# Laying k over its rows with 0/1 matmuls on four row tiles, in the projection of a fused attention and feed-forward layer

## The chip, the cores and the metric

The kernel runs on one core of a Trainium2 chip. The metric is the device time of one execution in microseconds (us); lower is better. Engine names are those of the profile: PE is TensorE (its weight loads are PEld), DVE is VectorE, ACT is ScalarE, POOL is GpSimd, and SP is SyncE, which here only issues DMAs (SPq is its queue).

## What is computed

The reference, cut to what matters here; the feed-forward half is only named.

```python
# x: (1, 4096, 256), 16 heads of 16
q = rope(x @ Wq.T + bq)         # per head; rope turns neighbouring features by a position's angle
k = rope(x @ Wk.T + bk)
v = x @ Wv.T + bv
p = softmax(q @ k.T / 16)       # per head, 4096 x 4096
x = layernorm(x + (p @ v) @ Wo.T)
x = layernorm(x + ffn(x))       # three gated and plain layers of width 1024
```

All of it is float32. Where a matmul is to be fast, an operand is split into a high part, rounded to the fp32r type, and a low part, the rest, and the products high by high, high by low and low by high are summed, as rows of one contraction.

## The kernel before

It has three stages that follow each other: `project`, `attend` and `feed_forward`. The change is in `project` and in the first waits of `attend`.

`project` goes over the sequence in NCH = 8 chunks of CH = 512 columns. A chunk has four items: q and k of feature half 0, then q and k of half 1 (item n, with t = n % 2 for q or k). For an item PE makes a 128x512 product into a PSUM bank `ps`, ACT adds the bias and writes `item[b]`, DVE swaps neighbouring rows into `pair` (a stream shuffle), multiplies `item` by the cosine table, POOL multiplies `pair` by the sine table, DVE adds the two (`rotated`), casts the sum to the high part (`high`) and subtracts to get the low part (`low`). After its four items a chunk's v is made: four token tiles, each two 128x256 float32 matmuls and a third with one row of ones that adds the bias of v.

What `attend` needs of k is `k_all`: for each pair of heads, 64 rows per head, in which rows 0 to 15 hold the high part, 16 to 31 the low part, 32 to 47 the high part again, and three rows of ones stand at 48 to 50 (`K_PART`, `SHIFT_ROW`). In the kernel before, SP stores both parts of q and of k into a DRAM tensor (`store`), and reads k's back into the three places per head (`place_k`: 6 DMAs for each chunk and half). The rows of ones are written by two DMAs at the start of `attend`. q is read back from DRAM later, in `attend`, by `place_q`.

The engines are separate programs, written as in-order lists with semaphores; nothing but these waits sets the order. DVE's `high` waits until the store that last used its `parts` buffer has landed (`parts_free`, line 288), SP's `place` waits for the landing of k's store, and SP's load of the next x and tables waits for `v_ready` and stands behind the chunk's stores and places on SP's list. PE's chunk waits for its x (`x_in`). `project` ends with SP's wait for all stores and for the places of k but the last, which `attend` issues.

`attend` begins with the `wide` matmuls (line 521) and DVE's maxima over them (line 710): these need the first q tile (`q_in`) and k.

Of the kernel before, what the change touches and what calls it, by code (L numbers as in the profile page):

```python
# [58 lines left out]
PLACES = PAIR * len(K_PART)  # L59


def place_k(sp, k_parts, k_all, c, ft, done):
    cols = bass.ds(c * CH, CH)
    pairs = slice(ft * PAIRS // FT, (ft + 1) * PAIRS // FT)
    for e in range(PAIR):
        for r, part in enumerate(K_PART):
            src = k_parts[part].rearrange("(j e d) s -> e d j s", e=PAIR, d=HD)[e]
            at = e * HALF + r * HD
            sp.dma_start(k_all[at:at + HD, pairs, cols].bitcast(F32), src[:, pairs, cols]).then_inc(done, 16)
# [10 lines left out]
def project(nc, io, parts_dram, v_all, k_all):  # L80

# [6 lines left out]
    with ExitStack() as ctx:  # L88
# [9 lines left out]
        RING = 4  # L98
# [3 lines left out]
        bv_sb = sb("b_v", [1, D])  # L102
        one_row = sb("one_row", [1, P])
        xt = [sb(f"xt{p}", [P, FT, CH]) for p in range(2)]
        table = [sb(f"table{p}", [P, 2, CH]) for p in range(2)]
        item = [sb(f"item{b}", [P, CH]) for b in range(RING)]
        pair = [sb(f"pair{b}", [P, CH]) for b in range(2)]
        parts = [sb(f"parts{b}", [P, 2, CH], F32R) for b in range(2)]
        ps = [psum(f"ps_qk{b}", [P, CH]) for b in range(RING)]
        psv = [psum(f"ps_v{a}", [P, 2, D]) for a in range(2)]  # L110

        w_in = sem("w_qk_in")
# [11 lines left out]
        low_done = sem("low_done")  # L124
        parts_free = [sem(f"parts_free{b}") for b in range(2)]
        k_in = sem("k_in")
        v_ready = sem("v_ready")
        v_free = sem("v_free")
        waited = sem("project_waited")
        sp_waited = sem("sp_waited")  # L130
        ones_set = sem("ones_set")

        ITEMS = 2 * FT
        TOTAL = NCH * ITEMS

        def started(n):

            return not isinstance(n, int) or 0 <= n < TOTAL

        block = ctx.enter_context(nc.Block())  # L140

        @block.sync
        def _(sp):
            def load(p, c):
                cols = bass.ds(c * CH, CH)
# [17 lines left out]
            def chunk(c, first=False):  # L163
                store(c, 0)
                if not first:
                    place(c - 1, 1)
                store(c, 1)
                store(c, 2)
                place(c, 0)
                store(c, 3)  # L170

            sp.dma_start(w_sb[:, 0], io["wqT"].rearrange("(t p) o -> p t o", p=P)).then_inc(w_in, 16)
            load(0, 0)
# [3 lines left out]
            sp.wait_ge(w_in, 16)  # L177
            sp.dma_start(w_sb[:, 1], io["wkT"].rearrange("(t p) o -> p t o", p=P)).then_inc(w_in, 16)
            sp.dma_start(wv_sb[:], io["wvT"].rearrange("(t p) o -> p t o", p=P)).then_inc(v_weights_in, 16)
            sp.dma_start(bv_sb[:], io["bv"].rearrange("(o d) -> o d", o=1)).then_inc(v_weights_in, 16)  # L180
            load(1, 1)
            chunk(0, first=True)
            sp.wait_ge(v_ready, 2)
            load(0, 2)
            chunk(1)
            sp.wait_ge(v_ready, 4)
            load(1, 3)
            with sp.Fori(1, NCH // 2 - 1) as cc:
                for p in range(2):
                    chunk(cc * 2 + p)  # L190


                    sp.wait_ge(v_ready, (cc * 2 + p + 1) * 2)
                    load(p, cc * 2 + p + 2)
            chunk(NCH - 2)
            chunk(NCH - 1)
            for b in range(2):
                sp.wait_ge(parts_free[b], 16 + 16 * TOTAL // 2)
            sp.wait_ge(k_in, 16 * PLACES * (NCH * FT - 1))

        @block.gpsimd
        def _(pool):
            pool.memset(v_all[:, :, :, :, HD:HD + 1], 1.0).then_inc(ones_set, 1)
            pool.wait_ge(ones_set, 1)
            pool.memset(one_row[:], 1.0).then_inc(ones_set, 1)
            pool.wait_ge(ones_set, 2)
            with pool.Fori(0, NCH // 2) as cc:
                for p in range(2):
                    pool.wait_ge(table_in[p], cc * 32 + 32)
                    for m in range(ITEMS):  # L210
                        n = (cc * 2 + p) * ITEMS + m

                        pool.wait_ge(swapped, n + 1)
                        pool.tensor_tensor(pair[m % 2][:], pair[m % 2][:], table[p][:, 1], ALU.mult).then_inc(sine_done, 1)

        @block.tensor
        def _(pe):
            def chunk(c, p):
                for m in range(ITEMS):
                    ft, t = m // 2, m % 2  # L220
                    n = c * ITEMS + m
                    if isinstance(c, int) and c == 0 and m < 2:

                        pe.wait_ge(w_in, 16 * (t + 1))
                    if started(n - RING):

                        pe.wait_ge(biased, n - RING + 1)
                    for i in range(FT):
                        last = pe.matmul(ps[m][:], w_sb[:, t, i, ft * P:(ft + 1) * P], xt[p][:, i],  # L229
                                         start=(i == 0), stop=(i == FT - 1))  # L230
                    last.then_inc(projected, 1)
                if isinstance(c, int) and c == 0:
                    pe.wait_ge(v_weights_in, 32)
                    pe.wait_ge(ones_set, 2)
                for a in range(2):

                    pe.wait_ge(v_free, c * 2 + a + 1)
                    for b in range(2):
                        tt = 2 * a + b
                        for i in range(FT):  # L240
                            pe.matmul(psv[a][:, b], xt[p][:, i, tt * P:(tt + 1) * P], wv_sb[:, i],
                                      start=(i == 0), stop=False)
# [4 lines left out]
            for p in range(2):  # L247
                pe.wait_ge(x_in[p], 16)
                chunk(p, p)
            with pe.Fori(1, NCH // 2) as cc:  # L250
                for p in range(2):
                    pe.wait_ge(x_in[p], cc * 16 + 16)
                    chunk(cc * 2 + p, p)

        @block.scalar
        def _(act):
            def chunk(c):
                for m in range(ITEMS):
                    ft, t = m // 2, m % 2
                    n = c * ITEMS + m  # L260
                    act.wait_ge(projected, n + 1)

                    act.wait_ge(low_done, n + 1)
                    act.activation(item[m][:], ps[m][:], ACT.Identity, bias=b_sb[:, t, ft:ft + 1]).then_inc(biased, 1)
                    if m >= ITEMS - 2:

                        a = m - (ITEMS - 2)
                        act.wait_ge(v_ready, c * 2 + a + 1)
                        for b in range(2):
                            dst = v_all[:, :, bass.ds(c * TT + 2 * a + b, 1), :, 0:HD]  # L270
                            last = act.activation(dst.rearrange("p g a j d -> p (g a) j d"),
                                                  psv[a][:, b].rearrange("p (g j d) -> p g j d", g=NG, j=HG), ACT.Copy)
                        last.then_inc(v_free, 1)

            act.wait_ge(b_in, 32)
            chunk(0)
            chunk(1)
            with act.Fori(2, NCH) as c:
# [1022 lines left out]
```

## Time and profile before

| what | value |
|---|---|
| median of 3 runs | 3553.01 us (3552.21 to 3554.25) |
| the profiled execution's own time | 3551.05 us |
| its span in the trace | 3549.4 us |
| mean granted clock of PE | 0.971 |
| busy: PE, DVE, ACT, POOL | 3414.3, 2997.2, 2451.1, 242.7 us |
| first matmul of `attend` | at 178.32 us |

The span is what the trace covers; the time is measured around it and is 1.65 us more. Every moment below is counted from the start of the span. The projection is the first twentieth of the span, and is the only stretch in which the DMA engines are nearly full; the page's forty slices of some 89 us each show that as the first two.

### The profile page before, as it was taken

To read this page: it belongs to the slowest core of one execution; us is meant where nothing else is said; L and a number is where in the kernel's file an instruction comes from. 1 tells how busy PE (TensorE), PEld (TensorE's weight loads), DVE (VectorE), ACT (ScalarE), POOL (GpSimd) and SP (SyncE) were. 2 spreads that over 40 slices of the span, in tenths; PEclk is the share of its full clock that TensorE was granted. 3 is DMA by queue.
4 is the path that set the end of the run, shared out by engine and by line. 5 is a ranking of instruction groups with operands and counts; after the bars stand their busy time and mean duration, and the time that the engine had idled before them with its cause. 6 is when DMAs were issued, how large, how long until landed. Compare 5 with 4: busy or idle time off the path is not lost. (4 is left out here: it accounts for less than half of the span.)

```text
span 3549.4 us, 67886 instructions
## 1 busy us (share of the span) xinstructions
PE 3414.3 (96%) x28122; PEld 1560.8 (44%) x28122; DVE 2997.2 (84%) x3204; ACT 2451.1 (69%) x4472; POOL 242.7 (7%) x440
## 2 busy tenths in 40 slices
PE   8569999999999999999999999999999699999998
PEld 3223333333333333333333333333333388888887
DVE  6599999999999999999999999999994245555554
ACT  2108888888888888888888888888889422222222
POOL 3300000000000000000000000000000011111100
PEclk8759999999999999999999999999999799999999
DMA  8920000000000010001000000000000501111100
GB/s 211 222 36 12 16 14 14 25 13 13 14 30 18 12 62 13 14 13 61 18 17 25 15 14 14 14 14 13 17 8 5 187 31 37 37 37 37 37 19 13
DMA packets 64150, 126.12 MB, mean 36 GB/s; under 512 B 13447, under 2 KB 25800, under 8 KB 62648
## 3 DMA queue, kind: packets, MB, share of 16 engines
q1 hardware_dynamic: 54920, 102.49, 10.3%
q0 software_dynamic: 8928, 19.35, 1.9%
q8 instruction: 221, 3.62, 0.4%
q14 instruction: 81, 0.66, 0.1%
HBM read 90.59 MB, written 41.16 MB: 37 GB/s over the span
## 5 line engine op out<-in xcount | busy, mean ns | idle before, releaser
L710 DVE TENSOR_REDUCE group_max<-wide 128x2 f32<-128x1024 f32 x2048 | 2473.0, 1222 | 23.9 <-PE wide L521 17.2
L681 ACT ACTIVATE probs<-scores 128x512 f32<-128x512 f32 x4046 | 2202.9, 600 | 291.8 <-PE scores L606 43.9
L547 PE MATMUL sums<-probs,v_all 128*17 128x256 f32 (+1 forms) x16120 | 1277.9, 389 | 7.7 <-ACT mixed L664 6.8
L606 PE MATMUL scores<-q_sb,k_all 51*128 51x512 f32 x3968 | 989.0, 495 | 6.7 <-ACT probs L681 5.7
L521 PE MATMUL wide<-k_all,q_sb 48*128 48x512 f32 x4096 | 850.6, 411 | 52.4 <-DVE group_max L710 26.7
L606 PEld LDWEIGHTS scores<-q_sb,k_all 51*128 51x128 f32 x3968 | 370.9, 183 | 843.5 <-ACT probs L681 830.0
L547 PEld LDWEIGHTS sums<-probs,v_all 128*17 128x17 f32 x16120 | 267.1, 95 | 748.1 <-issue 365.8
L521 PEld LDWEIGHTS wide<-k_all,q_sb 48*128 48x128 f32 x4096 | 397.8, 191 | 91.0 <-DVE group_max L710 63.9
L1083 ACT ACTIVATE whole_hid<-acc,scale 128x512 f32<-128x512 f32 x128 | 84.7, 689 | 321.7 <-PE acc L964 316.9
L964 PE MATMUL acc<-hid_b,h2T 128*128 128x512 f32 x1024 | 241.6, 396 | 0.0
L964 PE MATMUL acc<-hid_a,h1T 128*128 128x512 f32 x1024 | 240.2, 394 | 0.0
L964 PEld LDWEIGHTS acc<-hid_b,h2T 128*128 128x128 f32 x1024 | 192.3, 188 | 46.4
L964 PEld LDWEIGHTS acc<-hid_a,h1T 128*128 128x128 f32 x1024 | 191.6, 187 | 47.3
L1173 DVE CAST hid_a<-whole_hid 128x512 fp32r<-128x512 f32 x128 | 54.4, 425 | 185.7 <-ACT whole_hid L1083 183.5
L1074 ACT ACTIVATE gate<-acc,scale 128x512 f32<-128x512 f32 x64 | 44.1, 690 | 125.9 <-PE acc L964 125.9
L229 PE MATMUL ps_qk<-xt,w_qk 128*128 128x512 f32 x128 | 72.6, 729 | 27.7 <-DMA xt<-in_xT 27.6
L1175 DVE TENSOR_TENSOR hid_a<-whole_hid,hid_a 128x512 fp32r<-128x512 f32 x128 | 88.6, 692 | 4.4
L1182 DVE SCALAR_TENSOR_TENSOR whole_hid<-acc,scale,gate 128x512 f32<-128x512 f32 x64 | 48.1, 751 | 44.9 <-PE acc L964 44.9
L937 PE MATMUL tok<-wo,heads_sb 128*128 128x256 f32 x256 | 59.3, 392 | 17.8 <-DVE heads_sb L1148 17.8
L964 PE MATMUL acc<-x1t,w1T 128*128 128x512 f32 x256 | 71.8, 402 | 2.1 <-DVE x1t L1167 2.1
L1173 DVE CAST hid_b<-whole_hid 128x512 fp32r<-128x512 f32 x64 | 27.1, 424 | 55.1 <-ACT whole_hid L1083 55.0
L483 POOL CAST shift_parts<-shift 16x128 bf16<-16x128 f32 x32 | 8.9, 279 | 932.7 <-ACT shift L673 896.7
(89 smaller groups left out, 1295.0 us busy)
## 6 DMA issues: line engine op xcount, KB each, us to landing
k_all<-k_parts SPq DMA_DIRECT2D x96, 128.0 KB, 5.1
q_sb<-q_parts SPq DMA_DIRECT2D x192, 64.0 KB, 2.8
q_parts<-parts SPq DMA_DIRECT2D x16, 512.0 KB, 5.9
k_parts<-parts SPq DMA_DIRECT2D x16, 512.0 KB, 6.3
heads<-mixed SPq DMA_DIRECT2D x32, 256.0 KB, 2.6
heads_sb<-heads SPq DMA_DIRECT2D x8, 1024.0 KB, 4.9
shares<-shares_dram POOLq DMA_DIRECT2D x112, 64.0 KB, 2.3
xt<-in_xT SPq DMA_DIRECT2D x8, 512.0 KB, 6.3
```

The source lines that it names most:

```text
L229: last = pe.matmul(ps[m][:], w_sb[:, t, i, ft * P:(ft + 1) * P], xt[p][:, i], start=(i == 0), stop=(i == FT - 1))
L521: last = pe.matmul(wide[n % 2][:, e], q_sb[g][rows, j, t * P:(t + 1) * P], k_all[rows, g * GP + j, b * CH:(b + 1) * CH], start=True, stop= ...
L547: last = pe.matmul(sums[32 * j:32 * j + HD + 1, cols], v_all[:, g, kt, j], probs[(kt * HG + j) % RING][:, cols], start=(kt == 0 and cols.s ...
L606: pe.matmul(scores[(s + e) % BANKS][:], k_all[rows, g * GP + j, n // HG * P:(n // HG + 1) * P], q_sb[g][rows, j], start=True, stop=True).t ...
L681: act.activation(probs[n % RING][:], bank, ACT.Exp, scale=INV_SCALE)\
L710: dve.reduce_max(group_max[:, n], wide[n % 2][:], AX_X).then_inc(wide_free, 1)
L937: last = pe.matmul(tok[t // 2][:, t % 2], heads[:, g, t * P:(t + 1) * P], wo[:, g], start=(g == 0), stop=(g == NG - 1))
L964: mm = pe.matmul(dst, w.bitcast(view), src[h].bitcast(view), start=(first and h == 0), stop=(last and h == 1))
L1083: act.activation(whole[o % 4][:], acc[n % 4][:], ACT.Gelu, scale=scale[:, 2 + layer, o:o + 1])\
L1173: dve.tensor_copy(dst[0][:, k % HT], whole[k % 4][:]).then_inc(rounded, 1)
L1175: dve.tensor_tensor(dst[1][:, k % HT], whole[k % 4][:], dst[0][:, k % HT].bitcast(F32), ALU.subtract)\
L1182: dve.scalar_tensor_tensor(out=whole[o % 4][:], in0=acc[(2 * o + 1) % 4][:], scalar=scale[:, 1, o:o + 1], in1=gate[o % 2][:], op0=ALU.mult ...
```

## The change

`store` and `place_k` for k are gone, with k's DRAM tensor and the DMAs that wrote rows of ones. Instead PE lays k over its rows. A 0/1 matrix `choose` (32 rows by 128 columns for each of four pairs, for each of the two parts) says which row goes where; for each chunk and half (`spread_k`) PE runs eight fp32r matmuls of 128x512, two (high and low part) for each of four pairs, each with 32 rows, on the four row tiles of the array, into four PSUM banks. ACT copies each bank into `k_all`, adding a column `ones_rows` that is 1 in the three rows of ones. The k parts that the matmuls read lie in a stretch of `k_all` that is written last (`lent`).

Further: `ps` has two banks and not four; v's matmuls stand in the middle of a chunk, after items 0 and 1, and v's bias is one fp32r matmul with 128 rows (`two_rows`, `bv_parts`: high and low part of the bias) where a float32 matmul with one row stood; ACT copies v by one instruction for two token tiles; the high part is a tensor_tensor maximum of the item with itself and not a cast; the addition and the high part of item n come one item later on DVE, after the shuffle and cosine of item n + 1; the low part of q goes to POOL; all loops of `project` are written out; `v_all` has its axes in another order.

```diff
-            def store(c, m):
-
-                ft, t = m // 2, m % 2
-                sp.wait_ge(low_done, RING + c * ITEMS + m + 1)
-                dst = parts_dram[t].rearrange("a f s -> f a s")[ft * P:(ft + 1) * P]
-                sp.dma_start(dst[:, :, bass.ds(c * CH, CH)], parts[t][:].bitcast(F32)).then_inc(parts_free[t], 16)
-
-            def place(c, ft):
-
-                sp.wait_ge(parts_free[1], 16 + (c * FT + ft + 1) * 16)
-                sp.sem_inc(sp_waited, 1)
-                place_k(sp, parts_dram[1], k_all, c, ft, k_in)
...
+            for c in range(NCH):
+                for ft in range(FT):
+
+                    i = c * FT + ft
+                    sp.wait_ge(low_q, i + 1)
+                    dst = q_dram.rearrange("a f s -> f a s")[ft * P:(ft + 1) * P]
+                    sp.dma_start(dst[:, :, c * CH:(c + 1) * CH], parts[0][i % 2].bitcast(F32)).then_inc(q_stored[i % 2], 16)
+                if c + 2 < NCH:
+
+                    sp.wait_ge(v_ready, 2 * c + 2)
+                    sp.wait_ge(projected, (c + 1) * ITEMS)
+                    sp.wait_ge(rotated, (c + 1) * ITEMS)
+                    load(c + 2)
...
+            def spread_k(c, ft):
+                i = c * FT + ft
+                if i == 0:
+                    pe.wait_ge(choose_set, 5)
+
+                pe.wait_ge(low_k, i + 1)
+                if i > 0:
+
+                    pe.wait_ge(spread_free, JP * i)
+                for a in range(2):
+                    for j in range(JP):
+                        rows = slice(j * ROWS, (j + 1) * ROWS)
+                        last = pe.matmul(spread[j][:], choose[rows, a], parts[1][i % 2][rows, a],
+                                         start=(a == 0), stop=(a == 1))
+                        if a == 1:
+                            last.then_inc(spread_ready, 1)
+
+            for c in range(NCH):
+
+                pe.wait_ge(x_in[c % 2], (c // 2 + 1) * 16)
+                item_of(c, 0)
+                item_of(c, 1)
+                values(c)
+                if c > 0:
+                    spread_k(c - 1, 1)
+                item_of(c, 2)
+                item_of(c, 3)
+                spread_k(c, 0)
+            spread_k(NCH - 1, 1)
...
-                        last = pe.matmul(psv[a][:, b], one_row[:], bv_sb[:], start=False, stop=True)
+                        last = pe.matmul(psv[a][:, b], two_rows[:], bv_parts[:], start=False, stop=True)
...
+                for j in range(JP):
+
+                    act.wait_ge(spread_ready, i * JP + j + 1)
+                    act.activation(k_all[:, ft * JP + j, c * CH:(c + 1) * CH], spread[j][:], ACT.Identity,
+                                   bias=ones_rows[:]).then_inc(spread_free, 1)
...
+                dve.tensor_tensor(parts[t][i % 2][:, 0], item[n % RING], item[n % RING], ALU.max).then_inc(high_done, 1)
...
+                if n % 2 == 1:
+                    low(n - 1)
...
-            place_k(sp, k_parts, k_all, NCH - 1, FT - 1, k_in)
...
-            pe.wait_ge(k_ones, 16 * PAIR)
```

How the engines' lists look, at three places. PE in the kernel before, at the start of its first chunk (`ps_qk` are the items, `ps_v` is v):

```order
L229 MATMUL ps_qk<-xt,w_qk 128x512 x8
L241 MATMUL ps_v<-w_v,xt 128x256 x2
L244 MATMUL ps_v<-b_v,one_row 128x256
L241 MATMUL ps_v<-w_v,xt 128x256 x2
L244 MATMUL ps_v<-b_v,one_row 128x256
```

PE in the changed kernel, from the end of v in its second chunk on (`ps_spread` is k laid over its rows):

```order
L226 MATMUL ps_v<-b_v_parts,two_rows 128x256
L241 MATMUL ps_spread<-k_all,choose 128x512 x8
L208 MATMUL ps_qk<-xt,w_qk 128x512 x4
L241 MATMUL ps_spread<-k_all,choose 128x512 x8
L208 MATMUL ps_qk<-xt,w_qk 128x512 x4
L223 MATMUL ps_v<-w_v,xt 128x256 x2
```

The eight item matmuls of a chunk are now four and four, and behind each four and behind v stands work that needs what DVE has made of an earlier item.

ACT before, its first instructions after the table load:

```order
L264 ACTIVATE item<-ps_qk,b_qk 128x512 x3
L271 ACTIVATE v_all<-ps_v 128x4x4x16 x2
L264 ACTIVATE item<-ps_qk,b_qk 128x512
L271 ACTIVATE v_all<-ps_v 128x4x4x16 x2
L264 ACTIVATE item<-ps_qk,b_qk 128x512 x3
```

ACT in the changed kernel, its second chunk:

```order
L270 ACTIVATE item<-ps_qk,b_qk 128x512 x2
L277 ACTIVATE v_all<-ps_v 128x32x16 x2
L287 ACTIVATE k_all<-ps_spread,ones_rows 128x512 x4
L270 ACTIVATE item<-ps_qk,b_qk 128x512 x2
L287 ACTIVATE k_all<-ps_spread,ones_rows 128x512 x4
```

Four copies of k now stand on ACT ahead of the biases of items 2 and 3, and four more ahead of the next chunk's.

DVE before, for two items (item, cosine, high part of the item before, addition, low part of the item before):

```order
L305 STREAM_SHUFFLE pair<-item 128x512
L307 TENSOR_TENSOR item<-item,table 128x512
L289 CAST parts<-item 128x512
L311 TENSOR_TENSOR item<-item,pair 128x512
L294 TENSOR_TENSOR parts<-item,parts 128x512
```

DVE in the changed kernel, for an even item and the odd one after it:

```order
L354 STREAM_SHUFFLE pair<-item 128x512
L356 TENSOR_TENSOR item<-item,table 128x512
L310 TENSOR_TENSOR item<-item,pair 128x512
L321 TENSOR_TENSOR k_all<-item 128x512
L326 TENSOR_TENSOR k_all<-item,k_all 128x512
L354 STREAM_SHUFFLE pair<-item 128x512
L356 TENSOR_TENSOR item<-item,table 128x512
L310 TENSOR_TENSOR item<-item,pair 128x512
L321 TENSOR_TENSOR q_parts<-item 128x512
```

The low part of k (L326) is the fifth instruction of the iteration of the item after it, so that what PE lays out for a half of k waits for the bias of the next item.

## Rows read from the trace of the kernel before

In a row of stretches stand: from and to in us from the start of the span, its length, the busy us of PE, PEld, DVE, ACT and POOL (with the number of instructions), PE's granted clock as a share of full speed, the mean busy share of the 16 DMA engines, and GB/s.

**Rows 1.** Stretches of the span: two chunks of the projection, then the first maxima.

```profile
20.90:38.13 17.23, 13.68 (x41) 6.92 (x40) 15.64 (x26) 4.62 (x10) 7.19 (x5) 0.93 0.74 188
38.13:57.81 19.68, 15.83 (x40) 7.71 (x41) 13.31 (x26) 3.96 (x8) 7.08 (x4) 0.85 0.99 242
...
178.30:264.00 85.70, 59.34 (x151) 21.62 (x151) 84.71 (x78) 0.27 (x1) 2.95 (x7) 0.50 0.20 35
```

**Rows 2.** Waits from 0 to 180 us: total, times, longest.

```profile
DVE parts L289 <- DMA k_parts<-parts: 34.9, 14, 3.6
PE ps_qk L229 <- DMA xt<-in_xT: 27.6, 7, 5.5
```

**Rows 3.** PE's timeline in the projection: start us, us, engine, line, operation, count.

```profile
5.53 8.90 PE L229 MATMUL ps_qk<-xt,w_qk 128*128 128x512 f32 x16 [5.53 <-DMA xt<-in_xT]
...
20.90 7.13 PE L229 MATMUL ps_qk<-xt,w_qk 128*128 128x512 f32 x16
...
29.45 1.13 PE L241 MATMUL ps_v<-w_v,xt 128*128 128x256 f32 x4
30.51 0.69 PE L244 MATMUL ps_v<-b_v,one_row 1*128 1x256 f32 x2
31.14 1.13 PE L241 MATMUL ps_v<-w_v,xt 128*128 128x256 f32 x4
...
38.14 9.29 PE L229 MATMUL ps_qk<-xt,w_qk 128*128 128x512 f32 x16 [3.56 <-DMA xt<-in_xT]
...
77.45 10.10 PE L229 MATMUL ps_qk<-xt,w_qk 128*128 128x512 f32 x16 [3.42 <-DMA xt<-in_xT]
...
97.53 8.61 PE L229 MATMUL ps_qk<-xt,w_qk 128*128 128x512 f32 x16 [3.43 <-DMA xt<-in_xT]
```

**Rows 4.** DVE's timeline of one item.

```profile
22.42 0.71 DVE L305 STREAM_SHUFFLE pair<-item 128x512 f32<-128x512 f32 x1
23.17 0.69 DVE L307 TENSOR_TENSOR item<-item,table 128x512 f32<-128x512 f32 x1
23.78 1.49 DVE L289 CAST parts<-item 128x512 fp32r<-128x512 f32 x1
25.19 0.68 DVE L311 TENSOR_TENSOR item<-item,pair 128x512 f32<-128x512 f32 x1
25.79 0.68 DVE L294 TENSOR_TENSOR parts<-item,parts 128x512 fp32r<-128x512 f32 x1
```

**Rows 5.** DVE's timeline of the last item, the second waiting for the first.

```profile
163.56 0.43 DVE L289 CAST parts<-item 128x512 fp32r<-128x512 f32 x1 [3.56 <-DMA k_parts<-parts]
164.02 0.69 DVE L294 TENSOR_TENSOR parts<-item,parts 128x512 fp32r<-128x512 f32 x1
```

**Rows 6.** Groups by line and form, 0 to 260 us: busy us, mean ns of one, idle before.

```profile
L214 POOL TENSOR_TENSOR pair<-pair,table 128x512 f32<-128x512 f32 x32 | 56.6, 1769 | 99.7 <-DVE pair L305 99.7
L264 ACT ACTIVATE item<-ps_qk,b_qk 128x512 f32<-128x512 f32 x32 | 22.0, 689 | 60.4 <-PE ps_qk L229 59.1 <-DVE parts L294 1.2
```

**Rows 7.** Timeline of the feed-forward stage: three ACT instructions back to back.

```profile
2890.15 1.85 ACT L1083 ACTIVATE whole_hid<-acc,scale 128x512 f32<-128x512 f32 x3 [16.49 <-PE acc L964]
```

**Rows 8.** PE's timeline in attention: two pairs of fp32r matmuls, each pair on two row tiles.

```profile
600.28 0.50 PE L606 MATMUL scores<-q_sb,k_all 51*128 51x512 f32 x2
600.61 0.40 PE L521 MATMUL wide<-k_all,q_sb 48*128 48x512 f32 x2
600.94 0.63 PE L547 MATMUL sums<-probs,v_all 128*17 128x256 f32 x8
```

**Rows 9.** Timeline of the hand-over: the last store, the first q loads, the first matmul of attention.

```profile
166.28 0.43 SPq L155 DMA_DIRECT2D k_parts<-parts  x1
...
172.87 2.66 SPq L77 DMA_DIRECT2D q_sb<-q_parts  x6
...
178.32 1.22 PE L521 MATMUL wide<-k_all,q_sb 48*128 48x512 f32 x4 [25.76 <-DMA q_sb<-q_parts]
```

**Rows 10.** The page's DMA issues: size of one, median us from issue to landing.

```profile
k_parts<-parts SPq DMA_DIRECT2D x16, 512.0 KB, 6.3
```

More of the change, by code:

```diff
@@ L58 @@
 SLOT = SHIFT_ROW + 3
[L59 to L69, printed above, removed]
+PLACES = PAIR * len(Q_PART)
 def place_q(sp, q_parts, q_sb, c, g, done):
@@ L163, in chunk @@
[L163 to L173, printed above, removed]
+            sp.dma_start(w_sb[:, 0], io["wqT"].rearrange("(t p) o -> p t o", p=P)).then_inc(w_in[0], 16)
+            load(0)
@@ L181, in _ @@
[L181 to L196, printed above, removed]
+            for at in (0, ROWS):
+                sp.dma_start(bv_sb[at:at + 1], io["bv"].rearrange("(o d) -> o d", o=1)).then_inc(v_weights_in, 16)
@@ L216, in _ @@
+            for n in range(TOTAL):
+                c = n // ITEMS
+                if n % ITEMS == 0:
+                    pool.wait_ge(table_in[c % 2], (c // 2 + 1) * 32)
+                pool.wait_ge(swapped, n + 1)
+                pool.tensor_tensor(pair[n % 2], pair[n % 2], table[c % 2][:, 1], ALU.mult).then_inc(sine_done, 1)
+                if n % 2 == 1:
+                    low(n - 1)
         @block.tensor
         def _(pe):
[L218 to L234, printed above, removed]
@@ new lines, in item_of @@
+            def item_of(c, m):
+                ft, t, n = m // 2, m % 2, c * ITEMS + m
+                if c == 0 and m < 2:
+                    pe.wait_ge(w_in[t], 16)
+                if n >= BANKS:
+                    pe.wait_ge(biased, n - BANKS + 1)
+                for i in range(FT):
+                    last = pe.matmul(ps[n % BANKS][:], w_sb[:, t, i, ft * P:(ft + 1) * P], xt[c % 2][:, i],
+                                     start=(i == 0), stop=(i == FT - 1))
+                last.then_inc(projected, 1)
@@ L255, in _ @@
+            for c in range(NCH):
[3 more added lines that the diff above has]
+                values(c)
+                if c > 0:
+                    spread_k(c - 1, 1)
[3 more added lines that the diff above has]
+            spread_k(NCH - 1, 1)
         @block.scalar
         def _(act):
[L257 to L273, printed above, removed]
@@ L275, in _, with bias @@
-            act.wait_ge(b_in, 32)
-            chunk(0)
-            chunk(1)
-            with act.Fori(2, NCH) as c:
-                chunk(c)
-            act.wait_ge(v_free, 2 + 2 * NCH)
+            def bias(c, m):
+                ft, t, n = m // 2, m % 2, c * ITEMS + m
+                if n == RING - 2:
+                    act.wait_ge(bv_set, 3)
+                if n >= RING:
+                    act.wait_ge((low_q, low_k)[t], (n - RING) // 2 + 1)
+                act.wait_ge(projected, n + 1)
+                act.activation(item[n % RING], ps[n % BANKS][:], ACT.Identity, bias=b_sb[:, t, ft:ft + 1]).then_inc(biased, 1)
@@ L282, in _ @@
+            act.wait_ge(b_in, 32)
+            for c in range(NCH):
+                bias(c, 0)
+                bias(c, 1)
+                values(c)
+                if c > 0:
+                    spread_k(c - 1, 1)
+                bias(c, 2)
+                bias(c, 3)
+                spread_k(c, 0)
+            spread_k(NCH - 1, 1)
+            act.wait_ge(v_free, 2 * NCH)
+            act.wait_ge(spread_free, NCH * FT * JP)
         @block.vector
         def _(dve):
-            def high(n, b):
-                if started(n):
-                    dve.wait_ge(rotated, n + 1)
-                    dve.wait_ge(parts_free[b % 2], (n - b % 2) * 8 + 16)
-                    dve.tensor_copy(parts[b % 2][:, 0], item[b][:]).then_inc(high_done, 1)
@@ L291, in low, with rotate @@
-            def low(n, b):
-                if started(n):
-                    dve.wait_ge(high_done, n + 1)
-                    dve.tensor_tensor(parts[b % 2][:, 1], item[b][:], parts[b % 2][:, 0].bitcast(F32), ALU.subtract)\
-                        .then_inc(low_done, 1)
-            def chunk(c, p):
+            def rotate(n):
+                dve.wait_ge(cosine_done, n + 1)
+                dve.wait_ge(sine_done, n + 1)
+                dve.tensor_tensor(item[n % RING], item[n % RING], pair[n % 2], ALU.add).then_inc(rotated, 1)
@@ new lines, in high, with low @@
+            def high(n):
+                t, i = n % 2, n // 2
+                dve.wait_ge(rotated, n + 1)
+                if i >= 2 and t == 0:
+                    dve.wait_ge(q_stored[i % 2], 16 * (i // 2))
+                if i >= 2 and t == 1:
+                    dve.wait_ge(spread_ready, JP * (i - 1))
+                dve.tensor_tensor(parts[t][i % 2][:, 0], item[n % RING], item[n % RING], ALU.max).then_inc(high_done, 1)
+            def low(n):
+                k = parts[1][n // 2 % 2]
+                dve.wait_ge(high_done, n + 1)
+                dve.tensor_tensor(k[:, 1], item[n % RING], k[:, 0].bitcast(F32), ALU.subtract).then_inc(low_k, 1)
@@ L315, in _ @@
-            dve.sem_inc(v_free, 2)
-            for b in range(2):
-                dve.sem_inc(parts_free[b], 16)
-            for p in range(2):
-                dve.wait_ge(table_in[p], 32)
-                chunk(p, p)
-            with dve.Fori(1, NCH // 2) as cc:
-                for p in range(2):
-                    dve.wait_ge(table_in[p], cc * 32 + 32)
-                    chunk(cc * 2 + p, p)
-            high(TOTAL - 1, (TOTAL - 1) % RING)
-            low(TOTAL - 1, (TOTAL - 1) % RING)
```

169 lines of the change are left out of this document (97 added, 72 removed).

## The prediction

> **What bounds the kernel now.** The execution read here took 3551.05 us, 1.65 us more than its span, and lies 1.96 us under the median of the runs (3553.01). A measurement of this kernel can tell about 0.2%, some 7 us, from no change. The first question is which part of the span the change can reach. The stretches answer it: up to 152 us PE makes the projection, at 178.32 comes the first matmul of attention [rows 9], and from there on DVE is busy 84.71 of 85.70 us with its maxima [rows 1], an operation that the diff leaves alone. So I look for one number, the moment of that first matmul; all behind it moves by as much.
>
> Next, what a chunk of the projection lasts and why. The stretch from one chunk's first matmul to the next's is 19.68 us for the third chunk, with the DMA engines busy 0.99, PE 15.8, DVE 13.3 and ACT 4 us [rows 1]; three chunks in a row, from 38.14 to 97.53, take 19.8 us each [rows 3]. The waits name the same cause: DVE waits 34.9 us for the landing of k's stores, PE 27.6 us for x [rows 2]. One chunk shows the kernel before transfers crowd it: from 20.90 to 38.13, DMA share 0.74, 17.23 us, and 3.56 of these are PE's wait for x [rows 1, 3]. The projection is bound by its transfers, and a chunk without that bound needs 13.7 us of PE at full clock.
>
> Then the clock. It is 0.85 in such a stretch: after each wait of 3.4 to 3.9 us PE is at the lower of its two levels (1.2 GHz) for a while. A chunk's items take 7.13 us at 2.4 GHz (from 20.90) and 9.29, 10.10 and 8.61 after a wait [rows 3]; over the six chunks that begin after a wait the mean is 9.45. So a wait costs its own length and 2.3 us more.
>
> **What the change takes away.** Per chunk k's store is 1 MB (two of 512 KB [rows 10]) and its places are 1.5 MB, beside 1 MB of q's store and 1 MB of x and tables: 4.5 MB become 2. At the 240 GB/s of a full stretch that is 19 us before and 8.5 after. Transfers stop being the bound. Against that no term of the old chunk is left standing, so I build the new one from PE's list.
>
> **PE's work per chunk, at full clock.** Four items: one is a quarter of 7.13, that is 1.72 from start to start, 3.44 for two. v: per token tile the two matmuls take 1.06 (29.45 to 30.51) and the bias 0.63 (30.51 to 31.14) [rows 3]. The new bias matmul is fp32r with 128 rows; no such form is in the trace. It costs more than nothing and less than 0.63; the nearest row is one of the four records of 1.06, 0.265, and I take 0.25. v is then 4 x 1.31 = 5.24. Laying k out: eight matmuls on four row tiles. The nearest rows are pairs on two row tiles in attention: scores to wide and wide to sums are 0.33 us each for two matmuls of 512 columns [rows 8]. If four tiles run together, the eight cost 2 x 0.33 = 0.66; if only two do, 4 x 0.33 = 1.32; below 0.5 I see no reason, and I take 0.75, with something for changing the array's layout. Twice per chunk. Sum: 3.44 + 5.24 + 0.75 + 3.44 + 0.75 = 13.62 us, nearly what it was (13.7).
>
> Here a rule stands against the change. The rows with a one-row matmul among full ones already show such a price: 0.63 where the same columns with 128 rows take 0.53 [rows 3], so 0.1 us per change of layout, and my 0.75 holds that once. The Trainium skill, "TensorEngine Tiling (Array Packing)", section Key Properties, says that changing the tiling mode drains TensorE; by that the price would be paid going in and coming out, and the sum would be about 1.6 us longer over sixteen lays.
>
> **PE's new wait.** The order list puts the lay-out of a half right behind items 2 and 3, and it needs `low_k` of item 1. That is made on DVE in the iteration of item 2, which needs item 2's bias, and this stands on ACT behind four copies of k. From the end of the lay-out before items 2 and 3: 0.3 us until the first copy starts; four copies, one each 0.58 us (three in 1.85 us: (1.85 - 0.69) / 2 [rows 7]), 2.32; the bias 0.69 [rows 6] and 0.1 for its signal; then DVE: shuffle 0.75 and cosine 0.61 from start to start [rows 4], addition and high part 0.72 each, since each now waits for the one before (0.69 and a step of 0.03, as in [rows 5]), low part 0.69, with its signal 0.8. That is 0.3 + 2.32 + 0.79 + 3.6 = 7.0 us, under which PE has 3.44 us of items. PE waits about 3.6 us per chunk, and behind it in its list stands everything, the next chunk's items first. The wait for x is gone, but one of the same length takes its place. After a wait of 3.4 us the clock fell in each case seen, so I add the same 2.3 us. Period: 13.62 + 3.63 + 2.3 = 19.55 us, against 19.7 before.
>
> What else is on the lists hides under that. DVE per two items: two shuffles and cosines 2.72, two additions and high parts 2.9, one low part 0.7: 6.3, per chunk 12.6 of 19.6 us. The cast's 1.49 us [rows 4] goes, without gain, as DVE waits anyway; if the new form takes 1.49 too, the critical one before `low_k` does, and PE waits 0.8 us longer, 6 us in all. POOL does three instructions of 1769 ns [rows 6] per two items, 10.6 us per chunk; it would need 3.2 us each to matter. ACT: fourteen instructions of at most 0.69, 9.7 us. The loads of x are issued a chunk ahead and land in some 6 us; q's stores have their own buffers. The memsets and small DVE instructions of the start lie under the landing of the weights: I take v's first matmul at 11 us.
>
> **The sum.** First matmul at 5.53 as now. First chunk: items until 10.4, v until 16.2, items until 19.7, wait 3.2, lay-out: 18.5 us, so 24.0. Six chunks of 19.6: 141.6. Last chunk: 12.8 of PE, 2.3 for the clock, wait 3.7, a lay-out at the low clock 1.5, again a wait of 3.7 for the last low part, a lay-out 1.5, four copies 2.5: 28.0, so 169.6. Hand-over: before, the last store was issued at 166.28, with 6.3 us to landing [rows 10] that is 172.6 to 173.0, and the first q load was issued at 172.87 [rows 9]; I take 0.5. Then 5.45 us from the first q load to the first matmul (172.87 to 178.32), as before. That gives 175.6, where it was 178.32: 2.7 us earlier. 3551.05 - 2.7 = 3548.3, and with 1.96 for the median 3550.3 us. The change gives its own gain back through the new wait; what is left is the hand-over, in which k's last store no longer lands.
>
> **Rivals.**
> *A, likeliest: same within 0.2%.* The sum with the bounds of its small terms. The clock rises at moments that have to do with when the wait ends, and a chunk's loss was 1.5 us (8.61) to 3.0 us (10.10 [rows 3]); over eight chunks that is 6 us down or up. Chance 0.46, own range 3546 to 3560.
> *B, faster: the clock holds.* Items, v and lay-outs are denser than before, since no one-row matmul is among them. Then 2.3 us x 8 = 18 less: 3532. Against it: all seven waits of 3.4 us and more in the trace were followed by 1.2 GHz. Chance 0.12.
> *C, faster: small terms at their low ends.* Bias 0.15 and lay-out 0.6: 0.4 + 0.3 us per chunk, 5.6 us; with a wait of 3.3, 2.4 more: 3542. Chance 0.21. The Trainium skill's "TensorE: Matmul & The Clock Gate", Part 3, gives a speedup of 3.07 for four row tiles with 512 columns, which would favour this over two tiles at a time; no row of the trace has four tiles, so it changes no number here.
> *D, slower: row tiles do not run together.* At two at a time a lay-out costs 1.32, 0.57 more, and twice that at 1.2 GHz, where the one after the wait lies: 8 x (0.57 + 1.14) = 14 us: 3564. It decides from 1.0 us per lay-out on. Fully one after another (2.6) would be 3590. Chance 0.12.
> *E, slower: the wait is longer.* The new form of high part takes 1.49, or ACT's copies 0.69 each in a row: 0.4 to 0.8 us per chunk, up to 6 more, and a clock that rises later in every chunk: 3561. Chance 0.09.
> That the change does nothing since k's transfers were hidden is excluded for its first half by [rows 2]; what remains of it is A, in which their place is taken.
>
> **The numbers.** Faster (B, C) 0.33, same 0.46, slower (D, E) 0.21. The range takes A with C and most of D and E: 3538 to 3563.
>
> **What would show it.** In the changed kernel's stretches the DMA share of the projection falls to about 0.4. PE's waits name `low_k` (DVE's low part) once a chunk, 3 to 4 us, not x; its clock is again near 0.85. The period between two chunks' first matmuls is 19 to 20.5 us; a lay-out of eight takes 0.6 to 0.8 at 2.4 GHz; the fp32r bias 0.2 to 0.3; the high part 0.69. The first matmul of attention stands near 175.6. The prediction is wrong if PE's wait is under 2 us, if the clock stays up through it, or if the eight lay-out matmuls take more than 1 us.

## The result and the profile after

The changed kernel takes 3545.53 us (median of 20 runs, 3542.66 to 3549.1), the kernel before 3550.44 us in its 20 runs. The ratio is 0.9984, with a 95% interval of 0.9977 to 0.9991: some 5 us faster, within 0.2%, and clear of zero. The prediction was 3550 us (3538 to 3563) with "same" as the likeliest case. One execution of the kernel fill below took 5752.86 us and is left out of its median.

The profiled execution has a span of 3544.4 us where the kernel before had 3549.4. Its first matmul of attention is at 173.89 us where it was at 178.32 [rows 9]; behind it DVE is busy 84.73 of 85.70 us, as before [rows 1].

The timeline of PE in the changed kernel shows a chunk as a whole (start us, us, engine, line, operation, count, and the wait before it):

```profile
62.10 5.01 PE L208 MATMUL ps_qk<-xt,w_qk 128*128 128x512 f32 x8
...
67.92 1.03 PE L223 MATMUL ps_v<-w_v,xt 128*128 128x256 f32 x4
68.60 0.47 PE L226 MATMUL ps_v<-b_v_parts,two_rows 128*128 128x256 f32 x1
68.91 1.03 PE L223 MATMUL ps_v<-w_v,xt 128*128 128x256 f32 x4
...
70.97 0.74 PE L241 MATMUL ps_spread<-k_all,choose 32*128 32x512 f32 x8
71.64 3.70 PE L208 MATMUL ps_qk<-xt,w_qk 128*128 128x512 f32 x8
79.77 1.23 PE L241 MATMUL ps_spread<-k_all,choose 32*128 32x512 f32 x8 [4.43 <-DVE k_all L326]
80.92 5.83 PE L208 MATMUL ps_qk<-xt,w_qk 128*128 128x512 f32 x8
```

Read from item to item: the eight matmuls of items 0 and 1 take 5.0 to 5.8 us, v 0.98 us per token tile (67.92 to 68.91; 1.08 for the last one, which the lay-out follows), the lay-out behind it 0.67 (70.97 to 71.64), items 2 and 3 3.70; then PE waits 4.43 us for the low part of k, and the lay-out after the wait takes 1.15 (79.77 to 80.92). From 62.10 to 80.92 is 18.8 us. The six periods from 23.44 to 138.12 have a mean of 19.1 us. In the kernel before PE waited for x at this point [rows 2, 3].

Two of the waits from 0 to 176 us, as in [rows 2]:

```profile
PE ps_spread L241 <- DVE k_all L326: 39.4, 9, 5.7
...
PE ps_qk L208 <- DMA xt<-in_xT: 5.5, 1, 5.5
```

All of PE's waits for x but the very first are gone, 39.4 us for DVE's low part have come. The stretch of that chunk (columns as in [rows 1]):

```profile
62.10:80.92 18.82, 14.39 (x56) 7.76 (x52) 16.82 (x23) 8.68 (x14) 9.61 (x7) 0.86 0.33 112
```

The DMA engines are busy 0.33 where they were at 0.99, the clock is where it was (0.86, before 0.85), and DVE is busy 16.8 of 18.8 us. That last figure I had not expected: my sum had 12.6. DVE's and POOL's timelines at one place, where DVE ends one item and makes the next up to its low part:

```profile
90.92 0.69 DVE L356 TENSOR_TENSOR item<-item,table 128x512 f32<-128x512 f32 x1
91.53 1.76 DVE L310 TENSOR_TENSOR item<-item,pair 128x512 f32<-128x512 f32 x1
93.32 0.69 DVE L321 TENSOR_TENSOR q_parts<-item 128x512 fp32r<-128x512 f32 x1
94.48 0.01 DVE L354 LOAD_MASK_SELECT pair<-item  x1 [0.47 <-ACT item L270]
94.50 0.73 DVE L354 STREAM_SHUFFLE pair<-item 128x512 f32<-128x512 f32 x1
95.27 0.69 DVE L356 TENSOR_TENSOR item<-item,table 128x512 f32<-128x512 f32 x1
95.88 1.75 DVE L310 TENSOR_TENSOR item<-item,pair 128x512 f32<-128x512 f32 x1
97.66 0.69 DVE L321 TENSOR_TENSOR k_all<-item 128x512 fp32r<-128x512 f32 x1
98.39 0.69 DVE L326 TENSOR_TENSOR k_all<-item,k_all 128x512 fp32r<-128x512 f32 x1
```

```profile
90.97 1.77 POOL L193 TENSOR_TENSOR pair<-pair,table 128x512 f32<-128x512 f32 x1 [2.73 <-DVE pair L354]
94.10 1.27 POOL L186 TENSOR_TENSOR q_parts<-item,q_parts 128x512 fp32r<-128x512 f32 x1 [1.36 <-DVE q_parts L321]
95.33 1.75 POOL L193 TENSOR_TENSOR pair<-pair,table 128x512 f32<-128x512 f32 x1
```

The addition (L310), 0.68 us before [rows 4], takes 1.76: it begins while POOL multiplies by the sine table (90.97 to 92.74) and ends 0.55 us after POOL does. The shuffle beside POOL's low part (94.50) keeps its 0.73. PE and ACT at the same place, up to the lay-out that needs this low part:

```profile
91.27 3.70 PE L208 MATMUL ps_qk<-xt,w_qk 128*128 128x512 f32 x8
99.13 1.23 PE L241 MATMUL ps_spread<-k_all,choose 32*128 32x512 f32 x8 [4.16 <-DVE k_all L326]
...
91.38 2.42 ACT L287 ACTIVATE k_all<-ps_spread,ones_rows 128x512 fp32r<-128x512 f32 x4
93.67 0.70 ACT L270 ACTIVATE item<-ps_qk,b_qk 128x512 f32<-128x512 f32 x1
```

ACT's four copies do stand ahead of the bias of item 2 (93.67), but DVE has no time for that item before 94.01, when it ends the item before: it waits only 0.47 us for the bias.

The hand-over, in the timelines of ACT, SP and PE:

```profile
164.86 2.42 ACT L287 ACTIVATE k_all<-ps_spread,ones_rows 128x512 fp32r<-128x512 f32 x4 [4.58 <-PE ps_spread L241]
...
167.77 7.33 SPq L67 DMA_DIRECT2D q_sb<-q_parts  x16
...
173.89 1.22 PE L547 MATMUL wide<-k_all,q_sb 48*128 48x512 f32 x4 [9.16 <-DMA q_sb<-q_parts]
```

### The profile page after: what moved, and what is told of

It reads as the page before. It is cut to its first block and busy times, and to the rows that moved or that the text cites. A ratio compares the mean times of both kernels' runs of the same rounds, so it can differ in the third digit from the quotient of the medians.

```text
span 3544.4 us, 67661 instructions
## 1 busy us (share of the span) xinstructions
PE 3408.5 (96%) x28218; PEld 1563.6 (44%) x28218; DVE 3024.8 (85%) x3196; ACT 2488.0 (70%) x4520; POOL 263.8 (7%) x458
```

## The experiments

Ten kernels, each timed beside the kernel before on the same chip (its medians there 3550.3 to 3550.8 us); ratios are to those. Behind them stands a table with the first matmul of attention of each. Savings in us are against the changed kernel's 3545.53 unless the text says otherwise.

**1. Idle matmuls in PE's wait (fill).** The wait stays, but PE is busy in it.

```diff
+                if ft == 0:
+                    pe.wait_ge(v_free, c * 2 + 1)
+                    for _ in range(4):
+                        pe.matmul(psv[0][:].rearrange("p a d -> p (a d)"), w_sb[:, 0, 0, 0:P],
+                                  wv_sb[:].rearrange("p a d -> p (a d)"), start=True, stop=True)
                 pe.wait_ge(low_k, i + 1)
```

> The changed kernel with four float32 matmuls of 512 columns (0.86 us each at 2.4 GHz, 3.4 us) put on PE ahead of each lay-out of a chunk's first half, where PE waits 4.2 us; they write a bank that nobody reads. Theory: the wait costs its length and, through the clock, some 2 us for the items and 0.5 for the lay-out after it. With the wait filled the clock stays at 2.4 GHz, the wait itself stays (DVE's chain sets it): the period from chunk to chunk falls from 19.2 to about 16.8 us, the first matmul of attention comes 17 us sooner (near 157), the time is near 3528 where the changed kernel has 3545.5. Rival: the period is set by DVE or the copies and PE's clock is only a companion: no change, 3545.

Measured: 3534.92 us (median of five), ratio to before 0.9956 (0.9943 to 0.9969): 10.6 us less, where the theory had 17. In its trace of PE:

```profile
70.27 3.60 PE L237 MATMUL ps_v<-w_v,w_qk 128*128 128x512 f32 x8
74.87 0.74 PE L246 MATMUL ps_spread<-k_all,choose 32*128 32x512 f32 x8 [1.00 <-DVE k_all L331]
75.54 3.70 PE L208 MATMUL ps_qk<-xt,w_qk 128*128 128x512 f32 x8
```

After the filled wait the lay-out takes 0.67 and the items 3.70 us, in every chunk, where they took 1.1 and 5.6; the clock is 1.00 from 60 to 120 us. So the clock's part is shown: work that computes nothing saves 10.6 us. The period is 17.6 and not 16.8 us, though. From 22.67 to 128.41 DVE is busy 101.65 of 105.74 us, and it waits once a chunk, for 0.17 us:

```profile
83.56 0.72 DVE L359 STREAM_SHUFFLE pair<-item 128x512 f32<-128x512 f32 x1
84.31 0.69 DVE L361 TENSOR_TENSOR item<-item,table 128x512 f32<-128x512 f32 x1
84.92 1.76 DVE L315 TENSOR_TENSOR item<-item,pair 128x512 f32<-128x512 f32 x1
...
92.36 0.72 DVE L359 STREAM_SHUFFLE pair<-item 128x512 f32<-128x512 f32 x1
```

Two items in 8.8 us (83.56 to 92.36), 17.6 per chunk: with PE's clock up, DVE with its slow additions is the bound. The rival is half right.

**2. Lay-outs one chunk later (later).** On PE, and alike on ACT:

```diff
                 item_of(c, 1)
+                if c > 0:
+                    spread_k(c - 1, 0)
                 values(c)
                 if c > 0:
                     spread_k(c - 1, 1)
                 item_of(c, 2)
                 item_of(c, 3)
-                spread_k(c, 0)
```

> The changed kernel with both lay-outs of a chunk one chunk later, the first behind items 0 and 1 and the second behind v of the next chunk, on PE and on ACT alike. Theory: PE's wait for the low part of k is gone; DVE becomes the bound, with 8.3 us per two items (its addition takes 1.76 us while POOL works), 16.6 us per chunk; PE is busy 13.3. The first matmul of attention comes 12 to 17 us sooner, 3530. Rival: what bounds a chunk is DVE plus the transfer between engines in any order, then under 4 us: 3543.

Measured: 3543.67 us, 0.9982 (0.9973 to 0.9991), 1.9 us under the changed kernel, whose own runs lie apart by more. My theory fell. PE's wait did not go but moved behind v:

```profile
86.56 0.69 DVE L325 TENSOR_TENSOR k_all<-item 128x512 fp32r<-128x512 f32 x1
87.29 0.69 DVE L330 TENSOR_TENSOR k_all<-item,k_all 128x512 fp32r<-128x512 f32 x1
...
88.03 1.22 PE L241 MATMUL ps_spread<-k_all,choose 32*128 32x512 f32 x8 [3.95 <-DVE k_all L330]
89.19 9.52 PE L208 MATMUL ps_qk<-xt,w_qk 128*128 128x512 f32 x16
```

With its slow additions DVE needs some 17.6 us per chunk (fill), PE 12.2 at full clock. So PE waits in this order too, again in one piece, of 3.6 to 4.0 us, and the clock falls behind it (items 9.52 for 7.13); the period stays at 19.1 us. With more than one wait per chunk it can be otherwise (later_act, below).

**3. The bias of item 2 ahead of ACT's copies (bias2).**

```diff
                 values(c)
+                bias(c, 2)
                 if c > 0:
                     spread_k(c - 1, 1)
-                bias(c, 2)
                 bias(c, 3)
```

> The changed kernel with the bias of item 2 ahead of ACT's four copies of k's second half. My sum had 2.3 us of copies in PE's wait; if that holds the wait falls from 4.2 to under 2.5 us and the time by 13 us or more, since the clock gains too. Rival, from the trace after: DVE is busy until 0.3 us before that bias arrives, because its additions take 1.76 us, so the copies cost only 0.3 us per chunk: 3543, no change that can be told.

Measured: 3543.14 us, 0.9978 (0.9969 to 0.9987); PE's waits are 3.8 to 4.4 us, as they were. The 2.3 us of copies that my sum had in the wait cost next to nothing, as the rival had it: in the changed kernel DVE waits 0 to 0.94 us per chunk for the bias behind them, and it is not free earlier. That the median is 2.4 us lower is within what its runs lie apart. (Its profiled execution, with a span of 3549.4 us, lies above its median, so it is read here for the waits alone.)

**4. The kernel before without k's transfers (no_k).** What the removed transfers were worth by themselves. In their place `k_all` is filled by ACT with copies of a weight tile, and the waits for k's stores and places go too, so this kernel leaves out k, and its scores are not those of the reference.

```diff
                 store(c, 0)
-                if not first:
-                    place(c - 1, 1)
-                store(c, 1)
                 store(c, 2)
-                place(c, 0)
-                store(c, 3)
...
+                for j in range(PAIRS):
+                    act.activation(k_all[:, j:j + 1, bass.ds(c * CH, CH)].rearrange("p a s -> p (a s)"),
+                                   wv_sb[:].rearrange("p a d -> p (a d)"), ACT.Copy).then_inc(k_in, 1)
```

> The kernel before without k's stores and places (k_all is filled by ACT with copies of a weight tile, 4.5 us per chunk at its end; the scores are not those of the reference). Theory: transfers were the bound, and without them DVE is, at 3.97 us per item or 15.9 us per chunk, with PE's clock mostly high: the first matmul of attention comes at 145 to 150 us and the time is 26 to 33 us less, near 3521. Rival: the transfers of k were largely hidden and another wait sets the chunk: under 7 us less, 3545 or more.

Measured: 3520.21 us, 0.9916 (0.9903 to 0.9929), 30 us less than before. From its second chunk to its last (stretch, columns as in [rows 1]):

```profile
20.50:111.65 91.15, 84.67 (x242) 42.61 (x241) 90.36 (x139) 48.58 (x99) 40.22 (x24) 0.96 0.40 132
```

Six chunks in 91.15 us, 15.2 each, DVE busy 90.36 of them. So taking k's transfers away is worth 30 us, and the rest of the change costs 25 of the 30, though it has the cheaper bias of v (experiment 5) in it. PE still waits for x here in some chunks, and its clock falls behind waits shorter than those of the kernel before:

```profile
64.11 9.96 PE L222 MATMUL ps_qk<-xt,w_qk 128*128 128x512 f32 x16 [2.72 <-DMA xt<-in_xT]
...
111.65 10.09 PE L222 MATMUL ps_qk<-xt,w_qk 128*128 128x512 f32 x16 [2.34 <-DMA xt<-in_xT]
```

**5. v's bias as one row again (row1).** The changed kernel with the float32 matmul of one row.

```diff
-                        last = pe.matmul(psv[a][:, b], two_rows[:], bv_parts[:], start=False, stop=True)
+                        last = pe.matmul(psv[a][:, b], two_rows[0:1], bv_parts[0:1], start=False, stop=True)
```

> The changed kernel with v's bias again as one float32 matmul with one row, as before the change; all else as changed. The trace after shows 0.98 us per token tile where the kernel before took 1.69, so v would be 2.8 us longer per chunk. Theory: PE is on the path around the chunk (its wait starts when its own items are done), so the period goes from 19.2 to about 21.7 us and the time to 3560 to 3565, slower than the kernel before. Rival: DVE, with 16.5 busy us per chunk, takes most of it up: 3550 or less.

Measured: 3562.24 us, 1.0032 (1.002 to 1.0044): 17 us slower than the changed kernel and slower than the kernel before, as the theory had it. In its trace of PE a token tile takes 1.68 us again, from bias to bias (75.76 to 77.44):

```profile
74.80 1.03 PE L223 MATMUL ps_v<-w_v,xt 128*128 128x256 f32 x4
75.76 0.69 PE L226 MATMUL ps_v<-b_v_parts,two_rows 1*128 1x256 f32 x2
76.38 1.13 PE L223 MATMUL ps_v<-w_v,xt 128*128 128x256 f32 x4
77.44 0.69 PE L226 MATMUL ps_v<-b_v_parts,two_rows 1*128 1x256 f32 x2
```

This one small part of the change is worth more than the whole change brings. The edit turns back the rows (1 for 128) and the type (float32 for fp32r) together; no run separates them.

**6. The sine multiplication on DVE (sine_dve).**

```diff
-                pool.tensor_tensor(pair[n % 2], pair[n % 2], table[c % 2][:, 1], ALU.mult).then_inc(sine_done, 1)
...
+                    dve.tensor_tensor(pair[n % 2], pair[n % 2], table[c % 2][:, 1], ALU.mult).then_inc(sine_done, 1)
```

> The changed kernel with the multiplication by the sine table on DVE and not on POOL (q's low part stays on POOL). Theory: DVE's addition takes 1.76 us and not 0.69 because POOL's multiplication of the next item runs then; without it the addition is at 0.69 again, DVE's two items take 7.4 to 8 us and not 8.8, and in the order of the change PE's wait falls by about 0.5 us per chunk, with the clock still falling: 3538 to 3543. Rival: the addition is slow for another reason (its operands, its distance to the shuffle): it stays at 1.7 us, DVE has 0.6 us more per item, and the time is 3560.

Measured: 3539.12 us, 0.9966 (0.9954 to 0.9979), 6.4 us under the changed kernel although DVE has one instruction more per item. Groups on DVE from 0 to 130 us (busy us, mean ns, idle before):

```profile
L352 DVE TENSOR_TENSOR item<-item,table 128x512 f32<-128x512 f32 x27 | 18.7, 692 | 0.9
L353 DVE TENSOR_TENSOR pair<-pair,table 128x512 f32<-128x512 f32 x27 | 18.5, 685 | 0.0
L306 DVE TENSOR_TENSOR item<-item,pair 128x512 f32<-128x512 f32 x26 | 17.8, 684 | 0.0
```

The addition (L306) has a mean of 684 ns: it was POOL's multiplication that held it. PE's wait is 3.69 us, the clock still falls.

**7. Later, and nothing on POOL (later_dve).** The order of 2, with sine and q's low part on DVE.

> The kernel with both lay-outs one chunk later, and with sine and q's low part on DVE, so that POOL does nothing in the projection. Theory: DVE has 8.1 us per two items, 16.2 per chunk, all of them at 0.6 to 0.7, and is the only bound but for what the clock takes: period 16.5 to 18, first matmul of attention at 152 to 164, time 3525 to 3536. Rival: with PE 13.3 us busy and some 3 us idle in one piece the clock falls as before and the items behind it starve DVE: 19 us, 3543.

Measured: 3528.92 us, 0.9941 (0.9928 to 0.9955). PE's waits behind v are 2.4 to 3.2 us:

```profile
81.40 0.74 PE L233 MATMUL ps_spread<-k_all,choose 32*128 32x512 f32 x8 [2.42 <-DVE k_all L322]
82.06 7.13 PE L200 MATMUL ps_qk<-xt,w_qk 128*128 128x512 f32 x16
...
97.53 1.23 PE L233 MATMUL ps_spread<-k_all,choose 32*128 32x512 f32 x8 [3.22 <-DVE k_all L322]
98.69 9.68 PE L200 MATMUL ps_qk<-xt,w_qk 128*128 128x512 f32 x16
```

After 2.42 us the items take 7.13, after 3.22 us 9.68; two chunks of seven behind such a wait kept the clock throughout.

**8. The same with the high parts on ACT (later_act).** ACT copies `item` into the high part, DVE subtracts one iteration later.

> As the one with nothing on POOL, and with the high parts made by ACT (a copy) and the low parts one iteration later. DVE then has 6.6 us per two items, 13.2 per chunk, PE 13.3, ACT 11: no engine has an idle stretch of 3 us, so the clock stays up. Period 13.5 to 14.5, first matmul of attention near 138, time 3505 to 3512, faster than both kernels by 1%. Rival: the chain from bias to high part and low part through ACT's list (behind four copies) makes DVE and PE wait in turn: period 17 or more, 3530.

Measured: 3528.76 us, 0.9946 (0.9932 to 0.9959). The rival is right: the items of the middle chunks take 7.13, so the clock is up there, but the period is 16.8 us in five chunks of six and 18.2 in the other, since DVE waits 3.9 us per chunk (once 5.4) for a bias that stands behind copies of k on ACT's list. Less work on DVE and a longer chain make the same time.

**9. Sine on DVE and idle matmuls (sine_fill).** Edits 6 and 1 together.

> The changed kernel with the sine multiplication on DVE and the four idle matmuls in PE's wait, both of the edits that gained alone. Theory (two separate costs, POOL's hold on DVE and the clock after the wait): with the clock up PE's chunk is 3.4 + 3.9 + 0.7 + 3.4 + 0.7 and a wait of 3.7 us, 15.9 us, and DVE's at most 15.5, so the period is near 16 us where it is 18.5 with the sine edit alone and 17.6 with the idle matmuls alone; the first matmul of attention near 148, the time 3518 to 3524. Rival: the two are one cost seen twice: no better than the better of both alone, 3535.

Measured: 3525.14 us, 0.9927 (0.9913 to 0.994), the fastest that computes the reference: 25 us under the kernel before. The period is 16.3 us, in each chunk alike, and PE is busy 104.39 of 106.01 us (22.36 to 128.37), the idle matmuls with it. The two costs are not one cost seen twice: alone the edits gave 6.4 and 10.6 us, together 20.4. That is more than their sum, as in fill alone DVE's slow additions held the chunk at 17.6 us.

**10. The order of the change, nothing on POOL (all_dve).**

> The changed kernel in its own order with sine and q's low part on DVE, nothing on POOL. Against the one with the lay-outs one chunk later (3528.9) it tells what the order is worth once POOL is out of the way. Theory: the wait of 3.7 us behind items 2 and 3 is from the chain bias, shuffle to low part, not from POOL, and stays, with the clock: 3537 to 3541, as with the sine edit alone. Rival: the order is worth nothing here either, as it was worth nothing with POOL's hold: 3529.

Measured: 3539.84 us, 0.9968 (0.9956 to 0.998), as the theory had it: the same as with the sine edit alone. PE waits 3.7 us in each chunk from the third on. The later order was worth 2 us while POOL held DVE (experiment 2 against the changed kernel); it is worth 11 here (experiment 7 against 10).

| kernel | first matmul of attention, us | median, us |
|---|---|---|
| row1 | 191.44 | 3562.24 |
| before | 178.32 | 3550.44 |
| bias2 | 174.77 | 3543.14 |
| changed | 173.89 | 3545.53 |
| later | 172.16 | 3543.67 |
| all_dve | 168.86 | 3539.84 |
| sine_dve | 166.35 | 3539.12 |
| fill | 162.28 | 3534.92 |
| later_dve | 158.04 | 3528.92 |
| later_act | 157.59 | 3528.76 |
| sine_fill | 152.15 | 3525.14 |
| no_k | 147.37 | 3520.21 |

The median is that of all runs, the moment that of the one profiled execution. Their difference is 3370.8 to 3373.0 us in eleven of the twelve; in bias2, whose profiled execution is 7.9 us above its median, it is 3368.4. So the differences between the kernels arise ahead of that moment, and nothing behind it gives them back.

## Why the prediction was right

**What bounds and what moves.** Right. One number carried the result: 175.6 predicted, 173.89 measured, and the time followed it. The gain was 4.9 us where the sum had 2.7. The times themselves lie 4.8 us apart (3550.3 and 3545.53); 2.6 of these come from the three runs I started from, whose median was above that of the twenty. By stages: the first chunk took 17.9 us (18.5 in the sum), the six chunks 114.7 (117.6), the last up to the last copy 29.2 (28.0, since PE waits 5.67 us for the last low part and not 3.7), the hand-over 6.6 (5.95).

**What the change takes away.** Right, and no_k gives it its size: 30 us.

**The new wait.** Its place was right, behind items 2 and 3 and for the low part of k, and that it takes over from the wait for x. Its length was 4.16 to 4.43 us where I had 3.63, and the term that was mis-sized is DVE's chain. "Addition and high part 0.72 each" was for an addition with POOL idle; it takes 1.76, since the change puts it beside POOL's multiplication of the next item. In the chunk shown above, from the start of items 2 and 3 (91.27) to the shuffle (94.50) it is 3.2 us where the sum had 3.4, and from there to the lay-out (99.13) 4.6 where it had 3.6. ACT's copies stood in that chain as I had put them, but they did not set its length: DVE was busy with the item before nearly as long, so that moving the copies away gave no shorter wait (bias2).

I wrote that DVE had 12.6 us per chunk and that POOL would need 3.2 us per instruction to matter: fill shows 17.6 us of DVE per chunk with 0.17 us of wait in it, and sine_dve shows that POOL's multiplication of 1.77 us is the cause. Rows of before had held this: the cast of 1.49 us [rows 4] (23.78 to 25.27), which takes 0.43 at the end [rows 5], ran beside POOL:

```profile
23.21 1.77 POOL L214 TENSOR_TENSOR pair<-pair,table 128x512 f32<-128x512 f32 x1 [2.21 <-DVE pair L305]
```

The addition there never did, as it waited for that very multiplication.

The Trainium skill has the mechanism, in "SBUF — State Buffer", section "SBUF: two separate sides": VectorE and GpSimd share one pair of ports, an instruction with two SBUF inputs needs it against a GpSimd instruction that reads SBUF, and the one that comes second is blocked until the first is through. The traces agree, with 1.76 us beside POOL and 0.68 without. The cast has one input, so the rule as given here does not name it; that it is held too is what the trace shows.

**The clock.** Right in kind and in size. In the changed kernel items 0 and 1 after the wait take 4.69 to 6.30 us, 5.6 in the mean of seven, against 3.70, and the lay-out 1.06 against 0.67: 2.3 us per chunk, the figure of the sum. Fill takes it back in every chunk.

**PE's work.** The lay-out was at 0.75 and takes 0.67, so the row tiles work together (rival D is out). v was mis-sized: 5.24 predicted, 3.92 measured. I gave the new bias matmul 0.25, it takes 0.31, but the one-row matmul had cost more than its own 0.63: the two matmuls of 128 rows before it took 1.06 beside it and take 0.68 without. So some 0.4 us of what the one-row matmul cost stood in its neighbours' rows. I had put 0.1 us of it down to a change of the array's layout; no run tells that from the change of type. The step from v to the row tiles of the lay-out takes 0.1 us (the last token tile of v has 1.08 for 0.98), the step back shows none (0.67 is twice the 0.33 of [rows 8]). With both as measured PE's work is 13.62 - 1.32 - 0.16 + 0.1 = 12.2 us; with 4.3 for the wait, 2.3 for the clock and 0.26 by which items 2 and 3 end after the 3.44 that I gave them (3.70), the period comes to 19.1, as measured. That the predicted period of 19.55 lies so near was in part luck: v was 1.3 us too dear and the wait 0.5 to 0.8 us too short.

**The hand-over.** The 0.5 us between the last copy (167.28) and the first q load (167.77) was right; from there to the first matmul it takes 6.12 us, not 5.45.

**The rivals.** B, C, D and E did not happen; C's mechanism (cheaper small terms) is what v did, and E's (DVE slower than thought) came with another instruction than the one I named. A's class holds, but 3545.53 lies 0.5 us below A's own range of 3546 to 3560, towards C. What is not shown is how much of the 25 us that the change gives back belongs to each part: fill and sine_dve give 10.6 and 6.4 us alone and 20.4 together, and no kernel here lays out k without any cost.

## What to carry to other kernels

When a bound is removed, write the next one down from every engine's list, and look at which instructions of VectorE and GpSimd will newly stand beside each other; a duration read where the other engine was idle is not the duration beside it. A wait of TensorE costs its length and the half speed after it, so a change that swaps one wait of 4 us for another gains little. Filling such a wait, even with work that computes nothing, gives the second part back: 10.6 us here. A float32 operation of one row among full ones cost more here than its own row showed: price such a thing by the period of the whole group.

## What the runs showed that I had not expected

POOL's two-input 128x512 instruction takes 1.27 us when DVE has no two-input instruction running as it starts (q's low part), and 1.77 when DVE's cosine multiplication starts 0.05 us ahead of it; the mean of 1769 ns over the 32 of the kernel before [rows 6] is of the second kind, so about 0.5 us of it was probably a wait for DVE; no run here has POOL's multiplication alone.

A one-row float32 matmul of 256 columns makes a token tile 1.69 us where the fp32r one of 128 rows makes it 0.98: 0.7 us more. Its own step was 0.63, and the two matmuls before it took 1.06 where they take 0.68 beside the other: about 1.0 us in all.

The length of a wait alone did not tell whether the clock would fall. In later_dve it stayed up through waits of 2.42 and 2.46 us and fell behind one of 2.60 (items 8.83 us). In later_act it stayed up through most waits of 2.6 and fell behind one of them (a lay-out of 1.23 us at 57.75). In no_k it fell behind waits of 2.34 and 2.72 (items 10.09 and 9.96). In the projection it fell behind every wait of 2.89 us and more that items followed.
